# Making the first layer's second norm inside the attention loop of a two-layer transformer kernel

## The chip, the core and the metric

One core of one Trainium2 chip runs the whole kernel: TensorE (PE, matmuls and transposes), VectorE (DVE), ScalarE (ACT), GpSimd (POOL) and SyncE (SP, which issues DMAs), each with its own instruction stream, tied together by semaphores. The metric is device time in microseconds of one execution. Every number below is from one profiled execution of the kernel before, beside the median of three timed runs.

## The reference

x has 8 batches of 512 tokens of 256 values (4096 tokens). Two layers, each with an attention part and a mixture-of-experts part:

```
mod = silu(c) @ wmod                      # per batch: sa, ca, ga, sb, cb, gb
h = layernorm(x) * (1 + ca) + sa
x = x + ga * attention(h)
h = layernorm(x) * (1 + cb) + sb          # the "second norm"
x = x + gb * experts(h)
```

The first layer's attention is linear. With scalars q and k per token and head, cq = cos(tanh(q) pi/4) and sq the sine, ck and sk the same of k:

```
cos_KV = cumsum(ck * V); sin_KV = cumsum(sk * V)        # over the tokens of a batch
heads = (cq * cos_KV + sq * sin_KV) / (cq * cumsum(ck) + sq * cumsum(sk) + 1e-6)
out = W_O . heads                                        # 16 heads of 64 -> 256
```

The first layer's experts: logits = h @ router_w + b, the best 2 of 4 experts, each silu(h w1) * (h w3) @ w2. The second layer's: the best 1 of 8 experts, gelu(h W1) @ W2. Its attention is a 16-head softmax over small groups.

## The kernel before

The 4096 tokens are 32 tiles of 128 (NT = 32). Each matrix operand is a pair of float16 halves, "hi" (the value rounded) and "lo" (the rest), and a product is three float16 matmuls. ACT makes hi (a copy), POOL makes lo (a subtraction), or DVE where the source lies in PSUM.

**The stages in order.** Preparation and first norm; the attention loop over 32 tiles; the second norm of layer 0 (`pre_tick(0, t)`, 32 tiles in a software pipeline of seven steps) with the router's logits; routing; first experts (35 groups of 256 rows); merge; second attention; second norm of layer 1; second routing; second experts (39 tiles of 128 rows); combination. Each engine's program is written out by hand, so the order of calls in each engine function is the order of the instructions.

**One iteration i of the attention loop.** PE: `cum`, the running sum of cos_KV and sin_KV of tile i by a triangular matrix into PSUM banks 0 to 3 (8 matmuls, they wait for the lo halves kv_lo and for DVE's last reading `rd` of those banks); `turn_heads(i - 1)`, 8 transposes; `values(i + 2)`, V in two halves of 512 columns (12 matmuls); unless i % 4 is 3, the complement of the running sum (`atri`, 8 matmuls, after DVE's `rd` of tile i); `heads_out(i - 1)`, the output projection (24 matmuls). V and the projection's result share PSUM banks 4 and 5 in turn: the list `VR` gives the order, and `vr_free(u)` makes unit n wait until unit n - 2 has been read. So the projection of tile i - 1 waits until the first half of V of tile i + 2 has been spread.

DVE: four multiplications `rd` of the running sums by cq and sq (L1232, PSUM to SBUF, 512 columns each); `heads_lo(i - 1)`, two; `spread(i + 2)`, four products of V by ck and sk into KVF, two for each half of V; `hd`, the sum of both parts (1024 columns, two SBUF operands); `attended(i - 1)`: the projection's result by the gate (out of PSUM), the addition to X (two SBUF operands), the moments of X for the second norm, and every fourth tile `factor`. ACT: `heads_hi(i - 1)`, `spread_hi(i + 2)` (four copies of 512 columns), now and then a root, and `convert` of a piece of the expert weights (24 pieces, in i = 3 to 26). POOL: `spread_lo(i + 2)` (four subtractions of 512 columns), `convert` (one of 1024). SP issues the loads and stores of these pieces.

**The second norm, layer 0.** After the loop, for each tile: DVE makes h by two `scalar_tensor_tensor` (L1415, L1418) whose last operand, the modulation spread over partitions, lies in PSUM (`scale_rows`, PE, per batch); ACT rounds it; POOL subtracts; SP stores the row tile to HB in DRAM; PE turns it (4 transposes, L877); ACT copies it out of PSUM; PE multiplies by the router (6 matmuls of 4 columns). SP also starts the 32 pieces of the expert weights (WD to BIG) from row tile 22 on.

**Second experts.** POOL issues indirect DMAs: `fetch_weights(j)` (1 MB of up-projection weights, L2319, ring of 3), `fetch(1, t)` (128 rows of HB, L2284, ring of 4) and `put` (L2290, stores a result tile; it waits for ACT's copy of it). PE per tile j: up, `turn(j + 2)` (L1009, waits for the fetched rows), down(j - 1).

Of the kernel before, what the change touches and what calls it, by code (L numbers as in the profile page):

```python
# [22 lines left out]
w_hi w_lo th ck_hi ck_lo kc_ps dn V_ps kvf kv_hi kv_lo cum cum_b rd hd hdT_ps ht_hi ht_lo pr_ps yg cv_hi cv_lo  # L23
sc_ps hr hs_hi hs_hp hs_lo hT_ps hT lg_ps rw_hi rw_lo rt rt_a rt_p rt_ps it a1_a mp_ps
# [44 lines left out]
def program(nc, x_in, wqk_in, wv_in, wo_in, rw_in, rb_in, w1_in, w3_in, w2_in, c0_in, m0_in,  # L69
# [3 lines left out]
    with ctx:  # L73
# [107 lines left out]
        HT = area.pairs(2, 8, 128)  # L181
        pT, pc = bank(0, 2, 2, 8), bank(4, 12, 8)
# [25 lines left out]
        for i in range(NT):  # L208
            VR += [("v", i + 2, 0), ("v", i + 2, 1)] if i + 2 < NT else []
            VR += [("p", i - 1, 0)] if i else []  # L210
        VR += [("p", NT - 1, 0)]
# [7 lines left out]
        class Moe:  # L219
            def __init__(self, l, E, CH, w_rt, b_rt, gated):  # L220
# [20 lines left out]
                self.HR = area.ring(4, D)  # L241
                self.HP = area.ring(4, 2, D, dt=f16)
                self.HTR = area.ring(2, 4, 128, dt=f16)
# [72 lines left out]
        for n, total in dict(sc_ps=8, hr=2 * NT, hs_hi=NT, hs_lo=NT, hT_ps=NT, hT=NT, lg_ps=NT, rw_hi=1, rw_lo=1,  # L316
# [161 lines left out]
        def sync(e):  # L478
# [68 lines left out]
            sp.wait_ge(s["kc_ps"], 2)  # L547
            for c in range(CV[0]):
                convert(0, c)

# [11 lines left out]
            def rows_out(l, i):  # L562
                sp.wait_ge(s["hs_lo"], at(l, "hs_lo") + i + 1)
                e.dma_start(M[l].HBv[:, row_tile(l, i), :], M[l].HP[i % 4].rearrange(FLAT)).then_inc(st_hb[i % 4], 16)
                if l == 0 and i >= 22:
                    weights_in(0, i - 22)
# [17 lines left out]

            sp.wait_ge(s["rs_v"], 16)
            sp.wait_ge(s["pr_ps"], NT)
            router_in(0)
            for t in range(NT + 6):
                for k, i in steps(NT, 7, t):
                    if k == 2:  # L590
                        rows_out(0, i)
            for i in range(10, 32):
# [100 lines left out]
        def tensor(e):  # L693
# [48 lines left out]
            def vr_free(u):  # L742
# [5 lines left out]
                if kind == "v":  # L748
                    pe.wait_ge(s["kvf"], 4 * i + 2 * hf + 2)
# [75 lines left out]
            for i in range(NT):  # L825
# [28 lines left out]
                if i:  # L854
                    heads_out(i - 1)
            turn_heads(NT - 1)
            heads_out(NT - 1)

# [201 lines left out]
            pe.wait_ge(s["yg"], 2 * NT)  # L1060
            pe.wait_ge(s["modg"], 8)
            scale_rows(0, 0)
            for t in range(NT + 6):
                pre_tick(0, t)

            pe.wait_ge(s["hr"], 2 * NT)
            pe.wait_ge(s["hT"], NT)
# [1410 lines left out]
```

## Time and profile before

| | us |
|---|---|
| median of three runs (lowest, highest) | 1872.48 (1869.49, 1874.02) |
| the profiled execution's own time | 1872.36 |
| its span, first to last instruction | 1870.6 |
| attention loop, 66 to 397 us | 331 |
| second norm of layer 0, 397.9 to 439.2 us | 41.3 |
| routing of layer 0, 439.2 to 471.0 us | 31.8 |
| second experts, 1600 to 1832 us | 232 |

The span is cut by the time at which stages hand over. Over the whole span PE is busy 85%, DVE 63%, POOL 59%, ACT 47%; these shares are means over stages with different limits, so each stage is read by itself. In the timeline, a line is the start of a piece in us from the span's start, its length, the engine, the source line (most of DVE's `tensor_tensor` have the helper's line L1232, most of POOL's L2155, most of ACT's copies L1754, most of PE's matmuls L697) and the tiles; in brackets stands idle time of the engine before it, and what ended that.

### The profile page before, as it was taken

Reading aid. Unit: us, or ns where it says so; the run is one execution under the profiler, and the core shown is the slowest. Engines: PE = TensorE matmul, PEld = TensorE weight load, DVE = VectorE, ACT = ScalarE, POOL = GpSimd, SP = SyncE. Lnnn points to the kernel's source line nnn. Section 1 sums busy time; section 2 is a strip of 40 time slices with the busy share of each in tenths; the row PEclk is TensorE's granted clock in tenths of the full one; section 3 lists DMA queues with packets and bytes.
Section 4 is the critical chain, followed back from the end, with each engine's and each line's share of the span. In section 5 each row is a group of like instructions: output and inputs, shape, how many; then the busy total and the mean of one; then the engine's idle time right before and its main releaser. Section 6 shows DMA issues by size and latency. Waiting matters only on the chain.

```text
span 1870.6 us, 37951 instructions
## 1 busy us (share of the span) xinstructions
PE 1593.8 (85%) x13740; PEld 1175.0 (63%) x13740; DVE 1178.4 (63%) x1810; ACT 883.7 (47%) x1928; POOL 1108.3 (59%) x949
## 2 busy tenths in 40 slices
PE   6699999977999999999999458788888766899992
PEld 5455555555888888888888433234433235799882
DVE  7789998976333333333444486999999996222224
ACT  6544444444444444444544276444444335455553
POOL 5577787632333333333443498999997974455443
PEclk9899999985899999999999777999998976899996
DMA  5013233118333333323533420001111243566655
GB/s 204 23 46 114 94 109 113 46 49 312 97 103 103 103 100 100 95 92 93 161 118 91 133 81 1 23 26 27 29 29 57 74 137 101 206 238 226 224 200 188
DMA packets 118333, 204.13 MB, mean 109 GB/s; under 512 B 28480, under 2 KB 78672, under 8 KB 113040
## 3 DMA queue, kind: packets, MB, share of 16 engines
q1 hardware_dynamic: 102080, 132.22, 22.0%
q0 software_dynamic: 16080, 69.48, 10.6%
q8 instruction: 123, 2.02, 0.4%
q14 instruction: 50, 0.41, 0.1%
HBM read 138.09 MB, written 63.57 MB: 108 GB/s over the span
## 4 chain that ended last, share of the span: by engine, by line
PE 56%; POOL 15%; DVE 11%; issue 6%; DMA 6%; ACT 3%; SPq 0%; POOLq 0%; DVEq 0%; ACTq 0%
PE ps L697 53%; POOL BIG L2155 12%; DVE BIG L1232 6%; DMA BIG<-HB,BIG 3%; ACT BIG L1754 2%; DVE BIG L1703 1%; DMA BIG<-YT 1%; DMA HB<-BIG 1%; DVE X L1232 1%; POOL BIG L2352 1%; PE ps L940 1%; PE ps L811 1%; POOL X L2155 1%; DVE bnst L1239 1%; PE ps L1009 0%
## 5 line engine op out<-in xcount | busy, mean ns | idle before, releaser
L697 PE MATMUL ps<-BIG 128*128 128x256 f16 (+9 forms) x11272 | 1284.3, 287 | 129.0 <-DVE BIG L1681 46.6
L697 PEld LDWEIGHTS ps<-BIG 128*128 128x128 f16 (+3 forms) x11272 | 965.0, 101 | 413.2 <-issue 79.0
L2155 POOL TENSOR_TENSOR BIG<-BIG 128x512 f16<-128x512 f32 (+6 forms) x547 | 771.3, 1446 | 429.5 <-ACT BIG L1754 408.6
L1754 ACT ACTIVATE BIG<-BIG 128x512 f16<-128x512 f32 (+3 forms) x543 | 334.2, 628 | 296.6 <-DVE BIG L1232 263.5
L1232 DVE TENSOR_TENSOR BIG<-BIG 128x512 f16<-128x512 f32 (+9 forms) x334 | 267.8, 810 | 286.8 <-ACT BIG L1754 283.1
L1754 ACT ACTIVATE BIG<-ps 128x64 f32<-128x64 f32 (+7 forms) x799 | 281.0, 412 | 322.1 <-PE ps L697 216.6
L1232 DVE TENSOR_TENSOR BIG<-ps,BIG 128x512 f32<-128x512 f32 (+4 forms) x481 | 328.1, 743 | 42.2 <-PE ps L697 40.4
L1232 DVE TENSOR_TENSOR BIG<-BIG,ps 128x512 f32<-128x512 f32 (+2 forms) x212 | 125.1, 594 | 262.3 <-PE ps L697 245.9
L2290 POOL DMA_INDIRECT YT<-BIG x109 | 108.7, 998 | 199.2 <-ACT BIG L1754 198.6
L1703 DVE TENSOR_REDUCE BIG<-BIG 128x160 f32<-128x2560 f32 x64 | 184.5, 2882 | 0.0
L2284 POOL DMA_INDIRECT BIG<-HB,BIG x109 | 108.5, 995 | 62.8 <-DVE BIG L1232 31.5
L2068 ACT ACTIVATE ps<-ps 128x512 f32<-128x512 f32 x64 | 37.2, 582 | 137.1 <-PE ps L697 137.1
L1924 ACT ACTIVATE BIG<-ps 128x512 f32<-128x512 f32 x140 | 82.4, 588 | 12.1 <-PE ps L697 12.1
L1973 ACT ACTIVATE BIG<-ps 128x512 f32<-128x512 f32 x78 | 46.6, 598 | 42.2 <-PE ps L697 39.1
L697 PE MATMUL ps<-BIG,tri 128*128 128x512 f16 (+1 forms) x264 | 63.1, 378 | 0.9 <-ACT BIG L1781 0.9
L1681 DVE TENSOR_REDUCE BIG<-ps 128x32 f32<-128x512 f32 x64 | 44.1, 689 | 30.1 <-PE ps L697 29.5
L1239 DVE BATCH_NORM_STATS2 bnst<-X 128x6 f32<-128x256 f32 x128 | 54.6, 427 | 4.5 <-DMA X<-in_x 2.3
L2075 ACT ACTIVATE BIG<-ps 128x512 f32<-128x512 f32 x64 | 38.3, 599 | 37.9 <-DVE BIG L1703 37.9
L2319 POOL DMA_INDIRECT BIG<-WG,BIG x39 | 37.8, 970 | 28.8 <-DVE BIG L1232 13.5
L1087 PE MATMUL ps<-ident,BIG 128*128 128x128 f32 x64 | 17.8, 384 | 37.0 <-DVE BIG L1257 19.5
L697 PE MATMUL ps<-BIG,atri 128*128 128x512 f16 x192 | 45.4, 380 | 3.1 <-DVE BIG L1232 3.1
L2155 POOL TENSOR_TENSOR X<-X,BIG 128x256 f32<-128x256 f32 x48 | 33.3, 694 | 24.4 <-DVE BIG L1232 24.4
(133 smaller groups left out, 890.2 us busy)
## 6 DMA issues: line engine op xcount, KB each, us to landing
WD<-BIG SPq DMA_DIRECT2D x80, 256.0 KB, 2.5
BIG<-in_v SPq DMA_DIRECT2D x32, 512.0 KB, 4.4
BIG<-in_w SPq DMA_DIRECT2D x24, 512.0 KB, 4.0
BIG<-WD SPq DMA_DIRECT2D x32, 384.0 KB, 7.7
BIG<-YT SPq DMA_DIRECT2D x24, 512.0 KB, 4.9
HB<-BIG SPq DMA_DIRECT2D x64, 128.0 KB, 1.8
WG<-BIG SPq DMA_DIRECT2D x32, 256.0 KB, 3.2
BIG<-WD SPq DMA_DIRECT2D x16, 512.0 KB, 5.0
```

Source lines behind the costliest of these rows:

```text
L697: return e.matmul(o, lhsT, rhs, start=start, stop=stop, skip_group_check=True)
L1232: return e.tensor_tensor(o, a, b, op)
L1239: e.bn_stats(bnst[:, r, :], X[:, i, :]).then_inc(s["bn"], 1)
L1681: e.tensor_reduce(SM[q % 4], shaped(ps[2 + q % 3][:, :], (2, 16, 16)), AX.X, ALU.max).then_inc(s["sm"], 1)
L1703: e.tensor_reduce(OB[c % 2][:, 2 * q2:2 * q2 + 2], PV[q % 2], AX.X, ALU.add).then_inc(s["vr"], 1)
L1754: return e.activation(o, i, ACT.Copy)
L1924: e.activation(m_.UP[u % 2], ps[2 * u % 4][:, :], ACT.Silu).then_inc(s["su"], 1)
L1973: e.activation(m_.UP[j % 2][:, hf * 512:hf * 512 + 512], ps[idx % 4][:, :], ACT.Gelu).then_inc(s["su"], 1)
L2075: e.activation(PV[q % 2][:, :, :, 4, :], shaped(ps[2 + q % 3][:, :], (2, 16, 16)), ACT.Exp, scale=0.5).then_inc(s["e_sb"], 1)
L2155: return e.tensor_tensor(o, a, b, op)
L2284: e.indirect_dma_start(m_.HIN[t % ring], None, m_.HB, bass.IndirectOffsetOnAxis(m_.gi[:, t:t + 1], 0)).then_inc(ld_hi[t % ring], 16)
L2290: e.indirect_dma_start(m_.YT, bass.IndirectOffsetOnAxis(m_.yi[:, t:t + 1], 0), m_.YO[t % 2], None).then_inc(st_y[t % 2], 16)
```

## The change

1. In the attention loop DVE spreads both halves of V only for tiles 0 and 1; from tile 2 on it spreads the first, and ACT spreads the second by 16 copies of 64 columns with a scale per head (signal `kva`). ACT's and POOL's halves are then made in the order second half, first half.
2. The second norm of layer 0 is made in the loop: PE makes each batch's modulation rows at the end of iterations 3, 7, ..., 31 as a new unit ("s", b) in banks 4 and 5, ACT copies them to SBUF (`SC`); DVE's `rows(i - 5)` stands at the end of its iteration i, after `attended(i - 1)`; ACT's `rows_hi(i - 6)` and POOL's `rows_lo(i - 6)` stand at the head of theirs; SP's `rows_out(i - 6)` follows the conversion. The rows lie in `turned`, over the first norm's output, in four parts of 128 columns.
3. After the loop: the last tiles' rows, and for all 32 tiles only the transposes, the copies out of PSUM (ACT the even, DVE the odd ones) through a ring of three, and the logits. The pieces of the expert weights are loaded in another order: 11, 12 and 15 to 31 at the loop's end, 13 and 14 after the last rows are stored, 0 to 10 after the last transpose.
4. In the second experts POOL's `fetch(1, j + 3)` is issued ahead of `fetch_weights(j + 2)`.

The diff, cut to its core:

```diff
@@ tensor(e)
+                if i % 4 == 3:
+                    u = ("s", i // 4, 0)
+                    vr_free(u)
+                    pe.wait_ge(s["modg"], 8)
+                    by_batch(ps[4 + vr_no[u] % 2], 0, 2, 4, i // 4).then_inc(s["sc_ps"], 1)
+            def rows_turn(n):
+                pe.wait_ge(s["hs_lo"], n + 1)
+                if n >= 3:
+                    by, k = turned_by(n - 3)
+                    pe.wait_ge(s[by], k)
+                else:
+                    pe.wait_ge(s["rd"], 4 * NT)
+                for kk in range(4):
+                    m = e.transpose(bank16(1 + n % 3)[:, kk, :], turned[:, kk, 128 * n:128 * n + 128], ident16[:, :])
+                m.then_inc(s["hT_ps"], 1)
...
             turn_heads(NT - 1)
+            for n in range(3):
+                rows_turn(n)
             heads_out(NT - 1)
+            for n in range(NT):
+                logits(n)
+                if n + 3 < NT:
+                    rows_turn(n + 3)
@@ vector(e)
             def spread(i):
-                for hf in range(2):
+                for hf in range(1 if by_act(i) else 2):
...
+            def rows(n):
+                b = n // 4
+                dve.wait_ge(s["rs_v"], 8 + b + 1)
+                dve.wait_ge(s["sc"], b + 1)
+                if n >= 4:
+                    dve.wait_ge(s["hs_lo"], n - 3)
+                else:
+                    dve.wait_ge(s["dn"], 12)
+                h, sc = HR0[n % 4], SC[b % 2]
+                e.scalar_tensor_tensor(out=h, in0=X[:, n, :], scalar=stat[:, n, 0:1], in1=sc[:, 256:512],
+                                       op0=ALU.subtract, op1=ALU.mult).then_inc(s["hr"], 1)
+                dve.wait_ge(s["hr"], 2 * n + 1)
+                e.scalar_tensor_tensor(out=h, in0=h, scalar=rstd[:, n:n + 1], in1=sc[:, 0:256],
+                                       op0=ALU.mult, op1=ALU.add).then_inc(s["hr"], 1)
...
                 if i:
                     attended(i - 1)
+                if i >= R_AFTER:                 # R_AFTER = 5
+                    rows(i - R_AFTER)
             heads_lo(NT - 1)
...
+            rows(27)
+            router_lo(0)
+            rows_copy(1)
+            attended(NT - 1)
+            rows_copy(3)
+            factor(15, row(NT - 1))
+            for k in range(4):
+                rows(28 + k)
+                rows_copy(5 + 2 * k)
+            for n in range(13, NT, 2):
+                rows_copy(n)
@@ scalar(e)
+            def spread(i):
+                if by_act(i):
+                    act.wait_ge(s["V_ps"], 2 * i + 2)
...
+                    for j, q in ((0, QC), (1, QS)):
+                        act.wait_ge(s["kv_lo"], kv_no(i - 2, 1, j))
+                        for h in range(8):
+                            o = e.activation(KVF[i % 2][:, j, 512 + 64 * h:576 + 64 * h], ps[4 + vr_no["v", i, 1] % 2][:, 64 * h:64 * h + 64],
+                                             ACT.Copy, scale=q[:, i, 24 + h:25 + h])
+                        o.then_inc(s["kva"], 1)
...
             for i in range(NT):
+                if i % 4 == 0 and i:
+                    scale_rows(i // 4 - 1)
+                if i >= R_SPLIT:                 # R_SPLIT = 6
+                    rows_hi(i - R_SPLIT)
                 if i:
                     heads_hi(i - 1)
                 if i + 2 < NT:
+                    spread(i + 2)
                     spread_hi(i + 2)
@@ gpsimd(e)
             for i in range(NT):
+                if i >= R_SPLIT:
+                    rows_lo(i - R_SPLIT)
                 if i + 2 < NT:
                     spread_lo(i + 2)
...
                 for j in range(NS):
+                    if j + 3 < NS:
+                        fetch(1, j + 3)
                     if j + 2 < NS:
                         fetch_weights(j + 2)
-                    if j + 3 < NS:
-                        fetch(1, j + 3)
                     if j:
                         put(1, j - 1)
```

## Rows read from the trace of the kernel before

**Rows 1.** Windows by stage: us, busy us of each engine (instructions), PEclk, DMA share, GB/s

```profile
...
66.00:397.00 331.00, 301.20 (x1920) 186.22 (x1921) 298.72 (x497) 142.39 (x231) 230.95 (x153) 0.98 0.23 77
397.00:437.00 40.00, 26.89 (x371) 21.10 (x368) 29.95 (x70) 26.27 (x64) 19.85 (x32) 0.69 0.49 167
1600.00:1832.00 232.00, 221.07 (x2964) 204.74 (x2964) 54.02 (x78) 127.50 (x234) 110.18 (x113) 0.98 0.60 217
...
```

**Rows 2.** The same table, from the running sum of tile 2 to that of tile 31

```profile
97.63:384.85 287.22, 268.43 (x1674) 166.15 (x1672) 261.88 (x438) 124.62 (x202) 212.05 (x138) 0.99 0.26 85
```

**Rows 3.** Timeline of the attention loop, parts of three iterations

```profile
244.59 1.28 DVE L1232 TENSOR_TENSOR BIG<-BIG 128x1024 f32<-128x1024 f32 x1
246.87 1.41 DVE L1232 TENSOR_TENSOR X<-X,BIG 128x256 f32<-128x256 f32 x1
...
253.79 2.79 PE L697 MATMUL ps<-BIG 128*128 128x256 f16 x24 [0.49 <-DVE BIG L1232]
256.42 1.89 PE L697 MATMUL ps<-BIG,tri 128*128 128x512 f16 x8
256.62 0.42 DVE L1232 TENSOR_TENSOR BIG<-ps,BIG 128x256 f32<-128x256 f32 x1 [0.50 <-PE ps L697]
257.08 0.43 DVE L1232 TENSOR_TENSOR X<-X,BIG 128x256 f32<-128x256 f32 x1
...
258.35 6.07 DVE L1232 TENSOR_TENSOR BIG<-ps,BIG 128x512 f32<-128x512 f32 x10
...
265.96 1.89 PE L697 MATMUL ps<-BIG,tri 128*128 128x512 f16 x8
```

**Rows 4.** POOL's timeline in four short windows of the same stretch

```profile
243.62 1.16 POOL L2155 TENSOR_TENSOR BIG<-BIG 128x512 f16<-128x512 f32 x1 [1.63 <-ACT BIG L1754]
...
244.75 2.14 POOL L2155 TENSOR_TENSOR BIG<-BIG 128x512 f16<-128x512 f32 x1
...
246.84 2.46 POOL L2155 TENSOR_TENSOR BIG<-BIG 128x512 f16<-128x512 f32 x2
...
257.09 2.55 POOL L2155 TENSOR_TENSOR BIG<-BIG 128x512 f16<-128x512 f32 x2
```

**Rows 5.** Timeline of the merge, POOL beside DVE's scalar_tensor_tensor

```profile
1087.53 0.68 POOL L2155 TENSOR_TENSOR X<-X,BIG 128x256 f32<-128x256 f32 x1
1087.64 0.86 DVE L1637 SCALAR_TENSOR_TENSOR BIG<-BIG 128x256 f32<-128x256 f32 x1
```

**Rows 6.** Groups by form: busy us, mean ns; ACT over the span, POOL in the loop

```profile
L1754 ACT ACTIVATE BIG<-ps 128x64 f32<-128x64 f32 x256 | 44.3, 265 | 0.0
...
L2155 POOL TENSOR_TENSOR BIG<-BIG 128x1024 f16<-128x1024 f32 x24 | 51.5, 2145 | 4.1 <-ACT BIG L1754 4.1
```

**Rows 7.** Timeline around the second norm of layer 0

```profile
397.93 0.42 DVE L1232 TENSOR_TENSOR BIG<-ps,BIG 128x256 f32<-128x256 f32 x1 [2.37 <-PE ps L697]
...
418.40 0.30 PE L697 MATMUL ps<-BIG 128*128 128x4 f16 x6
418.63 0.40 PE L877 MATMUL ps<-ident,BIG 128*128 128x128 f16 x4
...
439.21 0.29 DVE L1232 TENSOR_TENSOR BIG<-ps,BIG 128x128 f32<-128x128 f32 x1 [7.28 <-PE ps L697]
```

**Rows 8.** Groups by form, 397 to 437 us

```profile
L1754 ACT ACTIVATE BIG<-ps 128x512 f16<-128x512 f16 x30 | 17.8, 595 | 1.0 <-PE ps L877 0.9
...
L1415 DVE SCALAR_TENSOR_TENSOR BIG<-X,stat,ps 128x256 f32<-128x256 f32 x32 | 15.2, 476 | 0.9 <-POOL BIG L2155 0.9
```

**Rows 9.** Who waited for whom, 1600 to 1832 us: us in total, times, longest

```profile
PE ps L1009 <- DMA BIG<-HB,BIG: 14.2, 10, 4.6
```

**Rows 10.** Timeline of the second experts

```profile
1730.47 0.97 POOL L2319 DMA_INDIRECT BIG<-WG,BIG  x1 [0.31 <-issue]
1731.74 0.95 POOL L2284 DMA_INDIRECT BIG<-HB,BIG  x1 [0.30 <-PE ps L1009]
1737.80 0.40 PE L1009 MATMUL ps<-ident,BIG 128*128 128x128 f16 x4 [1.12 <-DMA BIG<-HB,BIG]
```

More of the change, by code:

```diff
@@ L181, in program, with by_act, kv_no, kv_made @@
         HT = area.pairs(2, 8, 128)
+        SC = area.ring(2, 2 * D)
+        HR0 = [TH.rearrange("p t n -> p (t n)")[:, D * k:D * k + D] for k in range(4)]
+        turned = BIG16[:, 0:4 * T].rearrange("p (a t) -> p a t", a=4)
+        def by_act(i):
+            return i >= 2
+        def kv_no(i, hf, j):
+            return 4 * i + 2 * (hf if not by_act(i) else 1 - hf) + j + 1
+        def kv_made(i, hf, j):
+            if not by_act(i):
+                return "kvf", 4 * i + 2 * hf + j + 1
+            return ("kva", "kvf")[hf == 0], (8 if hf == 0 else 0) + 2 * (i - 2) + j + 1
+        R_AFTER, R_SPLIT = 5, 6
+        def turned_by(n):
+            return ("hT", "hT_d")[n % 2], n // 2 + 1
         pT, pc = bank(0, 2, 2, 8), bank(4, 12, 8)
@@ L1058, in gate_back @@
                 gate(1, 1, ps[3 + g % 3], g).then_inc(s["g_ps"], 1)
[L1060 to L1067, printed above, removed]
             routing(0)
@@ L1386, in vector @@
                     attended(i - 1)
+                if i >= R_AFTER:
+                    rows(i - R_AFTER)
             heads_lo(NT - 1)
-            attended(NT - 1)
-            factor(15, row(NT - 1))
             def router_lo(l):
@@ L1869, in router_hi, with rows_copy @@
                 copy(M[l].RW[0].rearrange(FLAT), M[l].RWf.rearrange(FLAT)).then_inc(s["rw_hi"], 1)
+            def rows_copy(n):
+                act.wait_ge(s["hT_ps"], n + 1)
+                if n >= 3:
+                    act.wait_ge(s["lg_ps"], n - 2)
+                copy(M[0].HTR[n % 3], bank16(1 + n % 3)).then_inc(s["hT"], 1)
+            router_hi(0)
+            rows_hi(26)
+            rows_hi(27)
+            rows_copy(0)
+            rows_copy(2)
+            root(2 * NT - 1, *row(NT - 1))
+            rows_copy(4)
+            for k in range(4):
+                rows_hi(28 + k)
+                rows_copy(6 + 2 * k)
+            for n in range(14, NT, 2):
+                rows_copy(n)
             def pre_tick(l, t):
@@ L2357, in merged @@
                 tt(X[:, i, :], X[:, i, :], M[0].YI[n // 4 % 3][:, 0, n % 4, :], ALU.add).then_inc(s["cb_x"], 1)
+            for n in range(NT - R_SPLIT, NT):
+                rows_lo(n)
             pool.wait_ge(s["rs_v"], 16)
-            for t in range(NT + 6):
-                pre_tick(0, t)
             routing(0)
```

110 lines of the change are left out of this document (73 added, 37 removed).

## The prediction

> **What bounds the kernel now.** I read the windows by stage first. In the attention loop PE is busy 301 and DVE 299 of 331 us, so neither share alone says what limits it; the clock is full. In the second norm no engine is above 75% and PE's clock stands at 0.69; the second experts keep PE at 95% [rows 1]. The 29 steps from the running sum of tile 2 to that of tile 31 take 287.22 us, 9.90 a tile [rows 2]. The timeline tells which engine sets a step [rows 3]. From the running sum at 256.42 to the next at 265.96 are 9.54 us with PE packed: that is PE's floor with the complement product. The step before, in which the addition to X took 1.41 us in place of 0.43, is longer, and there the projection (253.79) waits for DVE.
>
> So two loops run beside each other. DVE's goes through PE, and it is the one the change touches. Call DVE's first multiplication of an iteration 0. Ten operations of 512 columns take 6.07, or 0.607 each; the eighth, which spreads the first half of V, ends at 4.86 and frees the bank that the projection needs. The projection runs from about 4.9; DVE gets its result 2.83 later (253.79 to 256.62), at 7.74. Then come the gate, the addition to X, the moments: 256.62 to 258.35, of which 1.48 are work when the addition isn't held up and no factor is due. Sum 9.22, 0.3 under PE's 9.54. Held up by 0.98, the same loop takes 10.20. The mean of 9.90 is a mixture of the two [rows 2, 3].
>
> What holds it up is POOL. Its third subtraction began at 246.84, DVE's addition at 246.87, and the addition ended 0.43 after 247.85, which is 1.01 after POOL's start. In the other step DVE began at 257.08 and POOL at 257.09, and DVE took 0.43. The other way round too: POOL's second subtraction took 2.14 in place of 1.16 under DVE's 1024-column sum [rows 3, 4]. Whoever starts first keeps the other out for its operation: POOL's 512 columns for 1.01, DVE's 1024 for about 1.10, DVE's 256 for about 0.27 (256 of 1024 columns).
>
> **Part 1, half of the spreading moved to ACT.** DVE loses two operations, 1.21 us a tile. They stood between 4.86 and 6.07, while DVE waits for the projection until 7.74, so in DVE's loop they were hidden and their removal gives nothing; the wait grows. ACT gains 16 copies: 44.3 us for 256 such, 0.173 each, 2.8 us [rows 6]. At the mean length of one, 265 ns, not overlapped, they would take 4.2. With its other work (copies of 0.6 by the nearest form [rows 8]: two for the heads, four for V, one of 1.0 for the weights, one of 0.4 for the rows) ACT is busy 8 to 9.5 of a step, no bound. What its order does is set POOL's phase: rows (0.4), heads (1.1), 16 copies (2.8), first rounding (0.6): POOL can start at about 5.0.
>
> **Part 2, the rows in DVE's iteration.** They stand behind the moments and ahead of the next multiplications, on the one stretch of DVE's loop that is not covered. Two `scalar_tensor_tensor` of 0.476 [rows 8], issued 0.91 apart in sum, make the uncontended loop 9.22 + 0.91 = 10.13, above PE's floor. That is the lower bound of the step.
>
> Their last operand lay in PSUM and now lies in SBUF. With both operands in SBUF the nearest row is the merge's: such an operation began at 1087.64, 0.11 after a POOL addition, and took 0.86 instead of 0.48 [rows 5, 8]. So both new operations take part in the mutual exclusion, as the addition to X does. Walk one iteration: DVE's 1024-column sum starts at 4.86 and holds until 5.96; POOL's first subtraction follows to 6.97, the second runs 7.1 to 8.1, the third is due at 8.2. DVE's addition to X is due at 7.74 + 0.46 = 8.20. It is a race again.
> - DVE first: addition to 8.63, POOL's third 8.47 to 9.48, moments to 9.22, first row operation 9.48, POOL's fourth gets in at 9.75 and holds until 10.76, second row operation 10.76, next iteration at 11.2.
> - POOL first: addition at 9.21, POOL's fourth 9.48 to 10.50, first row operation 10.50, then POOL's weight piece of 1024 columns (2.15 us long [rows 6], holding about 2.0) 10.77 to 12.8, second row operation 12.8, next iteration at 13.25. Without a weight piece it would be 11.45.
>
> Weight pieces fall in 21 of the iterations with rows (6 to 26). I take the middle of the two branches, 12.2, since before the change the same race went about evenly; for the five other steps 11.3. Loop: 21 x (12.2 - 9.9) + 5 x (11.3 - 9.9) + 0.9 for the rows of the last iteration = 48.3 + 7.0 + 0.9 = +56.2 us.
>
> The Trainium skill (SBUF — State Buffer, section "SBUF: two separate sides") has a rule for this: VectorE and GpSimd share one port pair by an exclusive lock, taken for a whole instruction, and of VectorE's instructions with two inputs in SBUF take part against a GpSimd operation that reads SBUF. The trace agrees in all three places above (0.98 us lost by DVE, 0.98 by POOL, 0.38 in the merge). By the rule the moved operand alone brings the row operations in; without it the sum would end at the 1848 of the third rival.
>
> Hidden: PE's 8 matmuls per batch (0.6) lie under DVE's chain behind the projection, which is longer than the running sum by then; if not, 8 x 0.6. ACT's copies of them (0.6 per batch) and POOL's subtraction (0.64 a tile) fit in idle time; POOL comes to some 7.9 us of work in 12. SP's row stores now have pieces of 256 bytes; even at several times their former time, they are needed only by the first experts' fetch, tens of us later. The wait of ACT's `rows_hi` keeps `heads_hi` behind it until DVE's iteration ends: done at 1.5, needed at 2.43. A wait I can't price: PE now idles 2 to 3 us a tile, and PE's clock fell where it idled more [rows 1]; at the lower level a projection is 2.8 us longer, on the path. Bounds 0 and, in one tile of five, +15 us in all; taken 0.
>
> **Part 3, behind the loop.** Before: 397.93 to 439.21, 41.3 us [rows 7]. After, from the same point (the last projection): attended 1.5, then DVE's copy, factor and four pairs of rows and copy, about 0.6 + 0.25 + 4 x 1.5, then ten copies, one per two tiles. DVE's copy out of PSUM isn't in the trace; between 0.43 (256 columns) and 0.69 (512 with arithmetic), I take ACT's 0.595. A tile step: PE issues logits and transposes about 0.23 apart [rows 7], 0.46; the ring of three gives (0.23 + 0.40 + 0.6 + 0.1) / 3 = 0.44; with PE at its lower level near 0.6. I take 0.5. Sum 1.5 + 0.6 + 0.25 + 6.0 + 10 x 1.0 = 18.4, range 15 to 24. Gain 22.9 (17 to 26). The last weight pieces (11 of 32) start only after the last transpose; routing, some 30 us, covers them as it covered the tail of all 32 before; without that cover, up to 5 us.
>
> **Part 4, second experts.** Rows were issued at 1731.74 behind 1 MB of weights (1730.47) and PE waited for rows until 1737.80 [rows 10]. In all PE waited 14.2 us for rows, 4.6 of it once at the start, which the new order doesn't touch [rows 9]. Of the other 9.6 I take 8. The weights are issued 1.27 later; their tile is needed only after the next down product (2.7), so slack remains; if it doesn't, the gain is 0.
>
> **Sum.** +56.2 - 22.9 - 8 = +25.3 on the profiled execution's 1872.36 (span 1870.6 and 1.8 around it; the median is 1872.48): 1898 us.
>
> **Rivals.**
> - The race goes to POOL every time: 21 x 3.35 + 7.9 - 30.9 = +47, 1920 us. For it: once late, the order repeats itself. Against: before, it didn't.
> - The race goes to DVE every time: 21 x 1.3 + 7.9 - 30.9 = +4, 1877 us. Same evidence.
> - Faster: the row operations aren't held up, because POOL's later phase leaves them gaps or because they count like the PSUM form. Then the step is 10.13, 26 x 0.23 + 0.9 = +7, less 30.9: -24, 1848 us. The place is behind `attended`; it decides at a step of 11.0 or less, where the loop's loss no longer exceeds the 31 won elsewhere. Against: POOL is busy two thirds of the time, and [rows 5].
> - The rows are hidden altogether and the lighter DVE lets PE's 9.54 set the step: 26 x -0.36 - 30.9 = -40, 1832 us. It would need the rows off the path, where the order of instructions puts them on it.
>
> **Chances.** Mixture 0.42 (own range 1882 to 1912), POOL first 0.19, DVE first 0.17, rows not held up 0.17, hidden 0.05. A change within 0.3% (5.6 us, about what a measurement of this kernel can tell from none) comes mostly from "DVE first": same 0.13; faster 0.22; slower 0.65. Range 1848 to 1925.
>
> **What would show it.** Loop steps of 11 to 13.3 us while tiles 6 to 26 are in work, shorter behind them; DVE's new `scalar_tensor_tensor` stretched from 0.48 to 1 to 2.3 us, ended by a POOL operation; PE idle 2 to 4 us before the projection or running sum; the stretch from last projection to first routing operation 18 us; no wait for rows in the second experts after its start. I am wrong if the row operations keep 0.48 us, if steps stay under 10.5, or if PE waits for weights in place of rows.

## The result, and the profile after

The changed kernel takes 1911.26 us (1908.69 to 1913.57, four runs) against 1870.99 for the kernel before in the same session: it takes 1.0214 times as long, 95% interval 1.0191 to 1.0237. 1898 was predicted. The profiled execution took 1908.69.

In the fences, "..." marks lines left out; where a view is of several engines, lines of engines that play no part are left out without it.

The windows of the changed kernel, columns as in [rows 1], show the loop, the stretch of the norm that is left behind it, and the 29 steps from the running sum of tile 2 to that of tile 31:

```profile
66.00:466.00 400.00, 326.12 (x2002) 197.05 (x2003) 319.24 (x495) 246.05 (x750) 228.90 (x180) 0.92 0.24 72
466.25:484.20 17.95, 15.22 (x306) 13.23 (x302) 11.98 (x29) 10.38 (x20) 6.61 (x13) 0.81 0.83 306
96.60:451.62 355.02, 292.19 (x1730) 175.32 (x1728) 281.30 (x432) 221.22 (x685) 212.75 (x165) 0.92 0.26 78
```

287.22 [rows 2] became 355.02, 12.24 a step in place of 9.90: +67.8. The norm's stretch went from 41.28 [rows 7] to 17.9 (466.25 to 484.16): -23.4. From the first to the last row turn of the second experts there were 215.55 and are 205.06: -10.5. Smaller stretches (the loop's ends, routing, first experts) add 2.4, and the span went from 1870.6 to 1906.9, +36.3.

DVE's operations by form in the loop of the changed kernel (66 to 466 us; busy us, mean ns):

```profile
L1450 DVE SCALAR_TENSOR_TENSOR BIG<-BIG,rstd 128x256 f32<-128x256 f32 x28 | 34.3, 1227 | 1.0
L1301 DVE TENSOR_TENSOR X<-X,BIG 128x256 f32<-128x256 f32 x31 | 33.5, 1079 | 1.1
L1447 DVE SCALAR_TENSOR_TENSOR BIG<-X,stat,BIG 128x256 f32<-128x256 f32 x28 | 17.5, 624 | 0.2
```

The first and third are the row operations, 0.48 each when they stood alone [rows 8]. The second is the addition to X. The means hide that each takes a few lengths. Two iterations of the changed kernel's timeline:

```profile
236.49 1.89 PE L736 MATMUL ps<-BIG,tri 128*128 128x512 f16 x8
236.69 0.42 DVE L1301 TENSOR_TENSOR BIG<-ps,BIG 128x256 f32<-128x256 f32 x1 [1.76 <-PE ps L736]
237.15 1.32 DVE L1301 TENSOR_TENSOR X<-X,BIG 128x256 f32<-128x256 f32 x1
...
239.25 0.52 DVE L1447 SCALAR_TENSOR_TENSOR BIG<-X,stat,BIG 128x256 f32<-128x256 f32 x1
239.81 2.23 DVE L1450 SCALAR_TENSOR_TENSOR BIG<-BIG,rstd 128x256 f32<-128x256 f32 x1
241.96 4.86 DVE L1301 TENSOR_TENSOR BIG<-ps,BIG 128x512 f32<-128x512 f32 x8
...
244.49 3.26 PE L736 MATMUL ps<-BIG,atri 128*128 128x512 f16 x8 [2.65 <-DVE BIG L1301]
246.75 1.21 DVE L1301 TENSOR_TENSOR BIG<-BIG 128x1024 f32<-128x1024 f32 x1
247.32 3.88 POOL L2297 TENSOR_TENSOR BIG<-BIG 128x512 f16<-128x512 f32 x3 [4.09 <-ACT BIG L1852]
...
250.21 1.89 PE L736 MATMUL ps<-BIG,tri 128*128 128x512 f16 x8
...
252.47 2.30 POOL L2297 TENSOR_TENSOR BIG<-BIG 128x1024 f16<-128x1024 f32 x1
252.83 2.23 DVE L1450 SCALAR_TENSOR_TENSOR BIG<-BIG,rstd 128x256 f32<-128x256 f32 x1
...
259.90 4.35 PE L736 MATMUL ps<-BIG 128*128 128x256 f16 x24 [4.34 <-DVE BIG L1301]
264.29 0.42 DVE L1301 TENSOR_TENSOR BIG<-ps,BIG 128x256 f32<-128x256 f32 x1 [3.31 <-PE ps L736]
```

The second row operation takes 0.48, or 2.23 when POOL's weight piece of 1024 columns began just ahead of it (252.47 before 252.83). Of the 23 iterations from 160 to 450 us, 10 have it at 2.23. The addition to X takes 1.31 in 12 of them, 2.05 to 2.27 in four, and 0.42 to 0.86 in seven. The first row operation takes 0.70 in about half. The steps repeat in fours: 11.26, 13.72, 14.43, 11.24 from the running sum at 225.23 on.

In the short step of four the weight piece comes too late to hold anything:

```profile
225.89 1.31 DVE L1301 TENSOR_TENSOR X<-X,BIG 128x256 f32<-128x256 f32 x1
...
227.91 0.30 ACT L1858 ACTIVATE rstd<-stat,eps 128x4 f32<-128x4 f32 x1 [3.29 <-DVE stat L1310]
...
228.53 0.48 DVE L1450 SCALAR_TENSOR_TENSOR BIG<-BIG,rstd 128x256 f32<-128x256 f32 x1
...
229.23 2.75 POOL L2297 TENSOR_TENSOR BIG<-BIG 128x1024 f16<-128x1024 f32 x2 [1.02 <-ACT BIG L1852]
```

In every fourth iteration ACT makes a root ahead of its part of the weight piece, and waits for DVE's moments with it (3.29 idle). So POOL's piece begins 6.77 after DVE's sum of 1024 columns, not 5.72, and the second row operation, 6.07 after it, is free, though the addition was held to 1.31.

The two longer steps hold something else. Behind an idle stretch of 2.65 the complement product took 3.26 in place of 1.90, and behind one of 4.34 the projection took 4.35 in place of 2.79. The windows of a normal stretch of the changed kernel and of one such projection:

```profile
196.00:198.85 2.85, 2.85 (x26) 2.44 (x25) 0.45 (x1) 2.24 (x4) 2.85 (x3) 0.99 0.02 6
208.39:213.32 4.93, 4.93 (x24) 3.46 (x25) 1.07 (x1) 2.87 (x5) 4.49 (x4) 0.52 0.00 0
```

Granted clock 0.52, the lower of the two levels (1.2 GHz), after PE had idled 4.18. In the loop this befell six projections (13.1 us more than at full clock) and five complement products (7.3 more); in the kernel before, two projections in all.

In the second experts, who waited for whom (us in total, times, longest):

```profile
PE ps L1086 <- DMA BIG<-HB,BIG: 6.0, 2, 4.6
```

against 14.2 in ten waits [rows 9]; the 4.6 at the start is the same.

### The profile page after: what moved, and what is told of

The parts are those of the page before. It is cut to its first block, busy times and chain, and to the rows that moved or that the text cites. A ratio compares the mean times of both kernels' runs of the same rounds, so it can differ in the third digit from the quotient of the medians.

```text
span 1906.9 us, 38349 instructions
## 1 busy us (share of the span) xinstructions
PE 1605.1 (84%) x13740; PEld 1179.2 (62%) x13740; DVE 1180.3 (62%) x1766; ACT 968.2 (51%) x2400; POOL 1088.0 (57%) x949
## 4 chain that ended last, share of the span: by engine, by line
PE 57%; DVE 17%; POOL 12%; issue 7%; ACT 2%; DMA 2%; SPq 0%; POOLq 0%; DVEq 0%; ACTq 0%
PE ps L736 55%; POOL BIG L2297 10%; DVE BIG L1301 9%; DVE X L1301 2%; DVE BIG L1801 2%; DMA BIG<-YT 1%; ACT BIG L1852 1%; DVE bnst L1308 1%; DVE BIG L1447 1%; POOL BIG L2501 1%; PE ps L1017 1%; POOL X L2297 1%; DVE BIG L1779 1%; PE ps L1086 0%; DMA BIG<-HB,BIG 0%
## 5 line engine op out<-in xcount | busy, mean ns | idle before, releaser
L2297 POOL TENSOR_TENSOR BIG<-BIG 128x256 f16<-128x256 f32 (+6 forms) x547 | 751.6, 1406 | 488.1 <-ACT BIG L1852 466.9
L1852 ACT ACTIVATE BIG<-BIG 128x512 f16<-128x512 f32 (+3 forms) x543 | 329.9, 658 | 300.4 <-DVE BIG L1301 181.5
L1852 ACT ACTIVATE BIG<-ps 128x64 f32<-128x64 f32 (+7 forms) x791 | 275.5, 409 | 266.1 <-PE ps L736 236.2
L1301 DVE TENSOR_TENSOR BIG<-ps,BIG 128x512 f32<-128x512 f32 (+3 forms) x421 | 290.4, 745 | 82.0 <-PE ps L736 80.6
L1926 ACT ACTIVATE BIG<-ps,BIG 128x64 f32<-128x64 f32 x480 | 101.4, 368 | 12.4 <-PE ps L736 12.0
L2068 ACT ACTIVATE BIG<-ps 128x512 f32<-128x512 f32 x140 | 81.9, 585 | 12.1 <-PE ps L736 12.1
L736 PE MATMUL ps<-BIG,atri 128*128 128x512 f16 x192 | 52.8, 425 | 29.3 <-DVE BIG L1301 29.3
L736 PEld LDWEIGHTS ps<-BIG,atri 128*128 128x128 f16 x192 | 18.9, 107 | 61.3 <-DVE BIG L1301 38.4
L2468 POOL DMA_INDIRECT BIG<-WG,BIG x39 | 37.3, 955 | 27.0 <-DVE BIG L1301 13.5
```

The source lines that it names most:

```text
L736: return e.matmul(o, lhsT, rhs, start=start, stop=stop, skip_group_check=True)
L1301: return e.tensor_tensor(o, a, b, op)
L1852: return e.activation(o, i, ACT.Copy)
L1926: o = e.activation(KVF[i % 2][:, j, 512 + 64 * h:576 + 64 * h], ps[4 + vr_no["v", i, 1] % 2][:, 64 * h:64 * h + 64], ACT.Copy, scale=q[:, ...
L2068: e.activation(m_.UP[u % 2], ps[2 * u % 4][:, :], ACT.Silu).then_inc(s["su"], 1)
L2297: return e.tensor_tensor(o, a, b, op)
```

## The experiments

Each ratio is to the kernel before, timed on the same chip in the same session, with its 95% interval; the medians of the kernel before lie between 1870 and 1872 in all sessions, so differences between medians of two sessions are good to some 2 us. "Step" is the mean of the 29 steps between the running sums of tiles 2 and 31 in the one profiled execution, which lies 5.8 us below the median for a_conv, 4.2 above it for a_psum, and within 3 of it for the others.

### b_order: the kernel before, rows fetched ahead of weights

```diff
-                    if j + 2 < NS:
-                        fetch_weights(j + 2)
                     if j + 3 < NS:
                         fetch(1, j + 3)
+                    if j + 2 < NS:
+                        fetch_weights(j + 2)
```

> The kernel before with nothing changed but the order of POOL's issues in the second experts (rows ahead of weights). My theory: rows were late because 1 MB of weights lay ahead of them; the 12 us or so that separate the changed kernel's second experts from those before come from this alone: 8 to 11 us faster than before, PE's waits for rows there fall from 14.2 us to about 6 (the two at the start). Rival (the stage got faster because of what else changed, or one wait takes the other's place): no change, or waits for weights ahead of the up product.

Measured: 1859.84, ratio 0.9942 [0.9919, 0.9964], 12 us under the kernel before in its session. PE's waits for fetched rows are gone but for the start. Part 4 is worth 10 to 12 by itself (the interval allows 7 to 15), and PE doesn't wait for weights instead.

### b_spread: the kernel before with part 1 alone

```diff
-                for hf in range(2):
+                for hf in range(1 if by_act(i) else 2):      # DVE's spread, by_act(i) = i >= 2
...
+                    spread(i + 2)                            # ACT: 16 copies of 64 columns
                     spread_hi(i + 2)
```

The order of the halves and the waits that belong to part 1 are in it too.

> The kernel before with part 1 alone: ACT spreads the second half of V from tile 2 on; no rows in the loop. After the run with part 1 undone (33 us faster than the changed kernel, which I had not expected) two readings are open. My theory: in itself part 1 moves nothing on DVE's path; it shifts when POOL's subtractions fall, and without the rows only the addition to X can be held up: 1864 to 1880, steps of 9.5 and 10.2 in some mixture. Rival (ACT's chain, spread then rounding, makes POOL's halves late and so the running sum): slower by 10 us or more, with PE or DVE waiting for kv_lo.

Measured: 1862.37, ratio 0.9948 [0.9931, 0.9964]; step 9.50. That is just faster than the 1864 to 1880 expected. The addition to X takes 0.632 in the mean (0.854 in the kernel before), and nearly all steps stand at PE's floor of 9.49 to 9.54. My "removal gives nothing" was wrong even here: it ended the race of [rows 3], 0.4 a step. DVE doesn't win it. POOL begins some 0.8 ahead of the addition in every iteration (249.82 and 250.63), so the addition waits only for the last 0.2 of POOL's operation and takes 0.62, where it took 0.43 or 1.41.

### a_dve: the changed kernel without part 1

```diff
         def by_act(i):
-            return i >= 2
+            return False
```

> The changed kernel with part 1 undone: DVE spreads both halves of V again, ACT none; the rows stay in the loop. My theory: DVE's 1.21 us more lie in its wait for the projection, so the time is that of the changed kernel within 10 us, either way by where POOL's phase falls. Rival (ACT's 16 small copies made the loop slow): 25 us or more faster than the changed kernel. Rival (the spread given to ACT had been a gain that the rows ate up): 20 us or more slower.

Measured: 1877.85, ratio 1.0031 [1.0015, 1.0047], step 11.29. A miss: I had thought part 1 worth nothing with the rows in place, and it costs 33 us. The time is that of the first rival (ACT's 16 copies make the loop slow), but b_spread, where the same copies make the kernel faster, shows that they don't cost this by themselves. The same table as above, a_dve's loop:

```profile
L1450 DVE SCALAR_TENSOR_TENSOR BIG<-BIG,rstd 128x256 f32<-128x256 f32 x32 | 32.7, 1023 | 1.1
L1447 DVE SCALAR_TENSOR_TENSOR BIG<-X,stat,BIG 128x256 f32<-128x256 f32 x32 | 22.2, 695 | 0.3
L1301 DVE TENSOR_TENSOR X<-X,BIG 128x256 f32<-128x256 f32 x32 | 18.0, 562 | 1.1
```

and its timeline:

```profile
286.10 8.84 POOL L2297 TENSOR_TENSOR BIG<-BIG 128x512 f16<-128x512 f32 x6 [2.31 <-ACT BIG L1852]
287.08 1.27 DVE L1301 TENSOR_TENSOR BIG<-BIG 128x1024 f32<-128x1024 f32 x1
288.65 1.89 PE L736 MATMUL ps<-BIG,tri 128*128 128x512 f16 x8
...
289.31 0.42 DVE L1301 TENSOR_TENSOR X<-X,BIG 128x256 f32<-128x256 f32 x1
...
290.33 0.70 DVE L1447 SCALAR_TENSOR_TENSOR BIG<-X,stat,BIG 128x256 f32<-128x256 f32 x1
291.07 1.26 DVE L1450 SCALAR_TENSOR_TENSOR BIG<-BIG,rstd 128x256 f32<-128x256 f32 x1
```

POOL starts 0.98 ahead of DVE's sum of 1024 columns (286.10 and 287.08), gets one subtraction in, and the later ones fall so that the addition to X finds a gap: 20 of 24 take 0.42. With part 1 the sum comes 1.21 earlier in the iteration and POOL 0.36 later (ACT has its 16 copies to do first), so POOL starts 0.57 behind it (246.75, 247.32 above), and the addition is held in 16 of 23. That is the "DVE first" of the prediction with its step, 11.15 where nothing else intervenes (11.2 walked). That the total, 1877.85, meets the 1877 forecast is in part chance: four steps of 12.3 to 13.5 behind slow projections are in it.

### a_conv: the changed kernel, POOL's weight piece behind the next iteration's rows

```diff
+                if C_FIRST <= i - 1 < C_FIRST + CV[0]:
+                    convert(0, i - 1 - C_FIRST)
                 if i + 2 < NT:
                     spread_lo(i + 2)
-                if C_FIRST <= i < C_FIRST + CV[0]:
-                    convert(0, i - C_FIRST)
```

> The changed kernel, but POOL makes its weight piece (1024 columns) at the head of the next iteration, ahead of the V subtractions, where DVE has no operation with two SBUF operands. My theory (mutual exclusion; the weight piece gets in between the two row operations): the second row operation falls from a mean of 1.23 us to under 1.0, none over 1.5; steps of 13 us fall to about 11.3, the loop loses 1.2 to 1.9 us in each of 21 steps: 25 to 40 us faster than the changed kernel, near 1872 to 1886. Rival A (ACT's longer program sets the step): no change, since ACT and its waits stay as they are. Rival B (the extra product and the slower clock of PE set it): less than 8 us.

Measured: 1885.42, ratio 1.0072 [1.0055, 1.0089], step 11.27: 26 us won. The second row operation falls to 0.68 in the mean (1.23), the addition to X hardly changes (0.98). No 2.23 is left; POOL still goes first.

### dve_conv: both removals together

Both diffs, that of a_dve and that of a_conv.

> The changed kernel with both halves of V spread on DVE again, and POOL's weight piece (1024 columns, about 2.0 us of hold) moved behind the next iteration's row subtraction. The first alone gave 1878 (-33), the second alone 1885 (-26). Theory A (the two removals cure one and the same collision, the row operations against the weight piece, and what is left is the length of DVE's loop, 10.13, and X's addition): little is left to win, step 10.8 to 11.2, time 1865 to 1876. Rival (the two are separate costs that add, part 1 costing by PE's and ACT's timing and not by the weight piece): -33 and -26 add to 1852, step 10.3 to 10.5.

Measured: 1873.51, ratio 1.0013 [0.9997, 1.0028], step 11.07. -33 and -26 do not add to -59; together they give -38. Once DVE goes first, the piece is met seldom.

### a_psum: the last operand of the row operations in PSUM

```diff
+                elif 4 <= i <= 30:                    # PE, before it writes that bank again
+                    pe.wait_ge(s["hr"], 2 * (i - 4) + 2)
...
+                if n < 27:
+                    v = ps[4 + vr_no["p", n + 4, 0] % 2][:, 256:512]
+                    sc_a = sc_b = v
+                else:
+                    sc_a, sc_b = sc[:, 256:512], sc[:, 0:256]
```

The first row operation takes `sc_a` as its last operand, the second `sc_b`. PE's wait for the bank moves from the gate to the row operations, which can only make PE later.

> The changed kernel, but in the loop both row operations take their last operand from PSUM (the unused half of the projection's bank; the numbers there are not the modulation, so the rows of tiles 0 to 26 are other numbers). Work, order and waits stay. My theory: with one SBUF operand each they are no longer held up: 0.48 us each, while the addition to X still is in part of the tiles; step 10.1 plus about half of 1.0, so 10.6 in place of 12.2, about 45 us faster than the changed kernel (1860 to 1875). Rival (the row operations are slow for their place or their semaphore, not for the operand's place): durations and time as in the changed kernel. Rival (ACT sets the step): no change of time though the durations fall.

Measured: 1867.30, ratio 0.9973 [0.9961, 0.9986], step 11.02: 44 us faster than the changed kernel by the place of an operand (the rows of tiles 0 to 26 come out as other numbers here). The table for a_psum's loop:

```profile
L1303 DVE TENSOR_TENSOR X<-X,BIG 128x256 f32<-128x256 f32 x32 | 36.2, 1130 | 1.1
L1457 DVE SCALAR_TENSOR_TENSOR BIG<-BIG,rstd,ps 128x256 f32<-128x256 f32 x27 | 13.0, 481 | 1.0
L1454 DVE SCALAR_TENSOR_TENSOR BIG<-X,stat,ps 128x256 f32<-128x256 f32 x27 | 12.3, 457 | 0.2
```

0.46 and 0.48, never held up, with POOL busy beside them, while the addition to X (two SBUF operands) still pays 1.13 and keeps the step above the 10.6 expected. So the hold-up does depend on both tensor operands lying in SBUF, as the prediction took from [rows 3 to 5, 8]. By the Trainium skill (SBUF — State Buffer, "SBUF: two separate sides") VectorE and GpSimd share one port pair by an exclusive lock, in which a VectorE operation with two SBUF inputs takes part against a GpSimd operation that reads SBUF; this pair of kernels agrees (0.62 and 1.23 with both inputs in SBUF, 0.46 and 0.48 with one).

### a_hold: POOL's iteration waits until DVE's rows are done

```diff
+                if i > R_AFTER:
+                    pool.wait_ge(s["hr"], 2 * (i - 1 - R_AFTER) + 2)
+                ...            # then weight piece and spread_lo of the iteration before, then rows_lo
```

> The changed kernel with every instruction kept and one wait added: POOL starts its work of an iteration (weight piece, four V subtractions, rows) only when DVE has finished the rows of the iteration before, so that it runs while DVE reads PSUM. DVE's order is the changed kernel's, the rows stay on its path. My theory (mutual exclusion with POOL costs the loop 1.9 us a step beside the 0.91 of the rows): both row operations near 0.48 us, addition to X near 0.43, steps 10.1 to 10.6, 45 to 60 us faster than the changed kernel: 1850 to 1866. Rival (ACT, PE's clock or the rows' own time make the loop slow, and POOL's timing is a mere witness): no change, or slower, as POOL starts later.

Measured: 1853.33, ratio 0.9888 [0.9852, 0.9923], step 10.33. Row operations 0.51 and 0.46, addition 0.51; the lost time is now in DVE's sum of 1024 columns (1.70 in the mean in place of 1.24), which is partly hidden behind the projection. A wait added to POOL gains 58 us.

### a_early: the rows ahead of the wait for the projection

```diff
-        R_AFTER, R_SPLIT = 5, 6
+        R_AFTER, R_SPLIT = 6, 7
...
-                if i:
-                    attended(i - 1)
                 if i >= R_AFTER:
                     rows(i - R_AFTER)
+                if i:
+                    attended(i - 1)
```

> The changed kernel with the row operations ahead of `attended` in DVE's iteration, where DVE waits for the projection, one iteration later (rows(i - 6), rounding and subtraction at i - 7). No work is added or removed. My theory (the place behind the projection is the only uncovered one): the 0.91 us leaves the path, but POOL's first subtractions (from about 5.0) now get in between the 1024-column sum and the rows, so part of the hold-up stays: steps of 10.2 to 11.2, 30 to 55 us faster than the changed kernel (1855 to 1880). Rival (DVE's whole load sets the step): no change.

Measured: 1831.93, ratio 0.9780 [0.9746, 0.9814]: the fastest of all, 2.2% under the kernel before and 79 us under the changed one, better than the 1855 to 1880 expected. Step 9.61, clock 1.00. By form and in the timeline of a_early:

```profile
L1301 DVE TENSOR_TENSOR X<-X,BIG 128x256 f32<-128x256 f32 x32 | 19.6, 612 | 1.1
L1450 DVE SCALAR_TENSOR_TENSOR BIG<-BIG,rstd 128x256 f32<-128x256 f32 x32 | 16.4, 512 | 1.1
L1447 DVE SCALAR_TENSOR_TENSOR BIG<-X,stat,BIG 128x256 f32<-128x256 f32 x32 | 15.4, 480 | 0.0
```

```profile
259.20 1.62 DVE L1301 TENSOR_TENSOR BIG<-BIG 128x1024 f32<-128x1024 f32 x1
...
260.74 0.47 DVE L1447 SCALAR_TENSOR_TENSOR BIG<-X,stat,BIG 128x256 f32<-128x256 f32 x1
261.25 0.48 DVE L1450 SCALAR_TENSOR_TENSOR BIG<-BIG,rstd 128x256 f32<-128x256 f32 x1
261.86 7.40 POOL L2299 TENSOR_TENSOR BIG<-BIG 128x512 f16<-128x512 f32 x6 [2.13 <-ACT BIG L1853]
262.01 1.89 PE L736 MATMUL ps<-BIG,tri 128*128 128x512 f16 x8
262.21 0.42 DVE L1301 TENSOR_TENSOR BIG<-ps,BIG 128x256 f32<-128x256 f32 x1 [0.48 <-PE ps L736]
```

The rows stand while PE makes the projection (it ends at 262.2), and POOL, kept waiting by ACT's 16 copies, begins at 261.86, 0.13 after the second row operation has ended. The path behind the projection is rid of the rows, and the collision of nearly all it cost: the addition waits only for the last 0.2 of POOL's operation (0.62), and the sum of 1024 columns, held to 1.6 in most iterations by POOL's row subtraction begun at 259.06, ends while PE is still at the projection. PE sets the step now, 9.53 or 9.54, and 9.94 in every fourth, where the modulation rows stand ahead of the running sum. This is the prediction's "hidden" rival, 1832 us, reached by another order of instructions.

### x_free: a_early, POOL released by the addition to X

```diff
+                pool.wait_ge(s["yg"], 2 * i)
+                ...            # weight piece, then spread_lo(i + 2), then rows_lo
```

> Both at once: the rows ahead of `attended` (as in the run before the last), and POOL's iteration starting when DVE has made the addition to X, weight piece first. My theory: nothing of the rows is on the path and almost nothing is held up, so PE's 9.5 sets the step: loop 10 us shorter than in the kernel before, the norm's stretch 23 shorter, the second experts 10 shorter: 1825 to 1840, faster than both kernels. If the 1024-column sum is now held up by the subtractions by up to 1 us: 1840 to 1850. Rival: no better than the kernel before (1870).

Measured: 1849.61, ratio 0.9867 [0.9831, 0.9903], step 10.17. The addition is always free (0.43), and the time goes to the sum of 1024 columns (1.76) and the rows (1.01, 0.72). Protecting one operation moved the collision to the others; a_early's order without the wait is better.

### e_dve: a_early without part 1

Both diffs, that of a_early and that of a_dve.

> The changed kernel with the rows ahead of attended (as in the run that gave 1832, step 9.61), and both halves of V spread on DVE again, so without part 1. Theory A: DVE's work between its start and the projection's result is now 6.07 for ten operations, 1.10 to 1.28 for the sum of both parts and 0.95 for the rows, together 8.2 to 8.3, and the result is due at 7.74: 0.5 late, so part 1, worth 33 us the wrong way with the rows on the path, is here worth 0.5 a step the right way: step 10.0 to 10.3, time 1843 to 1853. Rival (part 1 costs whatever it stands beside, by ACT's later phase and PE's idling): 1832 or below.

Measured: 1889.86, ratio 1.0090 [1.0070, 1.0110], step 11.63. Both theories missed: part 1 is worth 58 us here, not 15. The timeline of e_dve:

```profile
251.30 5.30 PE L736 MATMUL ps<-BIG 128*128 128x256 f16 x24 [3.74 <-DVE BIG L1301]
251.38 8.76 POOL L2299 TENSOR_TENSOR BIG<-BIG 128x512 f16<-128x512 f32 x6 [2.98 <-ACT BIG L1853]
252.36 1.26 DVE L1301 TENSOR_TENSOR BIG<-BIG 128x1024 f32<-128x1024 f32 x1
253.54 1.38 DVE L1447 SCALAR_TENSOR_TENSOR BIG<-X,stat,BIG 128x256 f32<-128x256 f32 x1
254.95 1.26 DVE L1450 SCALAR_TENSOR_TENSOR BIG<-BIG,rstd 128x256 f32<-128x256 f32 x1
```

POOL starts at 251.38, ahead of sum and rows, and its subtractions alternate with them: the rows take 1.38 + 1.26 where I had put 0.95. DVE then has no idle time left and is the bound: in the iteration before this one its operations sum to 6.05 + 1.26 + 1.37 + 1.26 + 0.41 + 0.93 + 0.43 + 0.18 = 11.9, and the sums of 1024 columns lie 11.72 apart. I priced the removed operations and forgot what their removal does to POOL's start, the error of the prediction's part 1 once more, with the other sign.

### warm and warm_rd: PE kept busy ahead of the slow projection

```diff
+                if i % 4 == 3 and i >= 7:
+                    pe.wait_ge(s["rd"], 4 * i + 1)
+                    for r in range(13):
+                        m = mm(ps[0][:, :], tri[:, :], kv[0][:, 0, 0:512], True, True)
```

That is warm_rd; warm waited for `ht_lo` 2 * (i - 1) + 2 and ran 12 such matmuls into banks 6 and 7.

> The changed kernel, and in every fourth iteration (i % 4 == 3, from tile 7 on) PE fills its idle time ahead of the projection with 12 matmuls of 512 columns (about 2.8 us in a gap of 4.1 to 5.0) whose result nobody reads; they wait for nothing that the projection doesn't wait for. Six projections behind those gaps took 4.35 to 5.25 us in place of 2.79, together 13.1 more; five complement products behind gaps of 2.64 took 7.3 more and keep their gaps here. Theory A (PE's lower clock behind an idle stretch is on the path, and is worth 20 of the loop's +68): the six projections take 2.8, the loop is 12 to 14 us shorter, time 1896 to 1900. Theory B (the lower clock is only a companion; DVE and POOL set the step and the next wait takes the time back): projections shorter, the loop within 5 us of the changed kernel's, time 1906 to 1912.

Measured: 1913.41, ratio 1.0222 [1.0200, 1.0244]. The matmuls could start only at 259.04, 0.9 before the projection was due, took 0.43 each and let it begin 4.2 later. The projection itself took 2.96 in place of 4.35, so DVE had its result 2.5 later after its sum (7.0 in place of 4.5). The matmuls came behind the idle stretch and filled none of it, so this run doesn't tell the theories apart. It does show how little a delay costs: from the running sum at 249.86 to the one at 301.29 are 51.4 us, and in the changed kernel, from 250.21 to 301.13, 50.9: 2.0 of the 2.5 were given back within the same four steps.

> The changed kernel, and in every fourth iteration (i % 4 == 3, from tile 7 on) PE fills the gap ahead of the projection with 13 matmuls of 512 columns (about 3.1 us) into the bank that DVE's first multiplication of the iteration has just freed; nobody reads the result. The last attempt let them wait for the turned heads' halves, which came only 0.9 before the projection was due, so they delayed it by 4.2 and filled nothing. These can start about 0.8 after DVE's iteration begins and should end before the projection is due. Theory A (PE's lower clock behind an idle stretch is on the path): the six projections of 4.35 to 5.25 take 2.8, and the loop is 10 to 14 us shorter, time 1897 to 1902. Theory B (the time is taken back by the order of DVE's and POOL's operations, as the delay of the last attempt was): projections of 2.8, the loop within 5 us of the changed kernel's, time 1906 to 1913. If the projections stay over 4, nothing is told.

Measured: 1907.61, ratio 1.0189 [1.0167, 1.0211]. Its timeline:

```profile
254.60 2.98 PE L736 MATMUL ps<-BIG,tri 128*128 128x512 f16 x13 [0.84 <-DVE BIG L1305]
...
258.78 2.79 PE L736 MATMUL ps<-BIG 128*128 128x256 f16 x24 [1.20 <-DVE BIG L1305]
...
262.07 1.31 DVE L1305 TENSOR_TENSOR X<-X,BIG 128x256 f32<-128x256 f32 x1
...
264.72 2.23 DVE L1454 SCALAR_TENSOR_TENSOR BIG<-BIG,rstd 128x256 f32<-128x256 f32 x1
```

Every projection takes 2.78 to 2.99 now (2.79 here, clock 1.00 in its window), and though three complement products are slow where they weren't, some 14 us of slow time are gone; but the 29 steps take 351.75, only 3.3 less, as theory B had it. Counted from one DVE sum of 1024 columns to the next, the trace shows where the rest went:

- Four complement products were slow in the changed kernel and aren't now. They cost nothing: those steps take 13.0 to 13.1 with them and 13.0 without, since the weight piece holds the second row operation to the same time, whether the addition before it took 0.42 to 0.62 or 1.31.
- Five steps with a slow projection took 14.21 (four) and 13.34. There the weight piece came ahead of the addition or the first row operation. With a projection of 2.79 it meets the second row operation, and they take 13.0. That is 5.1 less.
- A sixth slow projection came behind the last weight piece, in a step of 12.21 that is 11.26 now: 1.0 less.
- Three of the short steps went from 11.26 to 12.1, the complement product ahead of them being slow now. That is 2.6 more.

So of 20 us of slow matmuls in the changed kernel some 6 were on the path. The addition is held in 22 of 23 iterations here (16 before) and the row operation has 2.23 in 15 (10), but by the first point that alone lengthens no step.

## Why the prediction was right, and where its sizes were off

- **The mechanism** stands: the row operations lie on the path behind `attended`, and they, like the addition to X, are held out by POOL because their operands lie in SBUF (a_psum, a_hold, a_early each remove it in another way and give 44, 58 and 79 us).
- **The two branches** were sized well. "DVE first" 11.2: 11.15 in a_dve. "POOL first" with a weight piece 13.25: from DVE's sum to its next one the long steps take 13.0 in the changed kernel and in warm_rd.
- **What chooses between them** is not the race that the prediction put there. The race wasn't even: POOL's third subtraction begins 3.3 after DVE's sum and the addition is due at 3.43, so while weight pieces last POOL wins by 0.1 whenever the projection is on time. And its winner doesn't set the step: with the addition held at 1.31 there are steps of 11.26 and of 13.02, and with it at 0.42 to 0.62 there are steps of 13.0 as well. The step is long when the weight piece begins (5.72 after the sum) ahead of the second row operation (6.08), short when ACT's root puts it off to 6.77.
- **The loop's term**, +56.2, measured +67.8. The step was taken as 12.2 for the 21 iterations with a weight piece (6 to 26), and they took 12.85 in the mean. Five are short (11.26), eleven long (13.0), and five are those with a slow projection (14.21 and 13.34). Sixteen of 21 beyond the short length, not half, make some 8.4 of the 13.6 missing there; the slow projections on top of 13.0 make the other 5.1, where the prediction had put "bounds 0 and +15; taken 0". The steps outside the 21 came 2 us cheaper than taken. That 12.2 came this close is in part luck: half and half was right for neither the reason nor the share.
- **"In DVE's loop they were hidden and their removal gives nothing"** (part 1) is the step that failed, though not in the total. Their time was hidden; their place set when DVE's sum and POOL's subtractions begin. Measured: -10 alone, +33 beside rows behind `attended`, -58 beside rows ahead of it. Its 16 copies took 3.38, where 2.8 had been taken, within the bound of 4.2. The 0.173 behind it was a misreading of [rows 6]: those 256 copies come in pairs, a pair busy for 0.35, and say nothing of a row of 16. POOL, put at "about 5.0" in the iteration, began at 5.36 (247.32 less 241.96).
- **The norm's stretch**, -22.9, measured -23.4. DVE's copy out of PSUM is 0.42, not the 0.595 taken from ACT; with PE's clock lower in the middle (a transpose 0.59 in place of 0.38) a pair of tiles took 1.17 there and 0.75 to 0.86 later, around the 1.0 taken.
- **Second experts**, -8, measured -10.5; b_order shows it by itself.
- **Hidden edits**: the rows' rounding and subtraction cost nothing that shows: POOL's takes 0.67 in its idle time, and ACT's rounding for the heads is done 1.5 after DVE's iteration begins (242.39 + 1.06 against 241.96), as worked out. PE's modulation rows cost nothing where DVE sets the step; in a_early, where PE does, they show as 9.94 in place of 9.54.

## What to carry to other kernels

Before costing a step in a loop where two engines exclude each other, write down when each one's block of operations starts, and ask what every edit does to these starts: an operation whose time is hidden may still be the spacer that keeps two blocks apart. Short added work belongs into the stretch where its engine waits anyway, ahead of the waiting instruction. Where it must meet the other engine all the same, an operand in PSUM kept it at its own length here.

## What the runs showed of the hardware

- DVE's operations of 256 columns with two SBUF operands took 0.42 to 0.48 free, 1.26 to 1.31 when issued just behind the start of POOL's 512 columns, and 2.23 just behind 1024. When they came later in POOL's operation they took what was left of it and their own time: 0.62 (the addition in b_spread and a_early) and 0.70 (the first row operation in half the iterations of the changed kernel).
- The length of one idle stretch did not tell whether PE's next product was slow. In the changed kernel it was after 4.1 to 5.0 of idling (six of six) and after 2.64 (four of five); in a_dve after 3.17 (four of six); in warm_rd never after 2.64, but after 2.19 (three of five). 13 matmuls whose result nobody reads, ahead of every fourth projection, kept all projections at 2.78 to 2.99.
- 16 copies of 64 columns out of PSUM in a row, with a scale of their own per partition, began 0.20 apart on ACT and took 3.38 in all.
